# Places of weight and operand tiles modulo 512 bytes in stage 3, and a wait of GpSimd at the end of stage 2

## The reference

```python
def _cross_attention(q_in, kv_in, wq, bq, wk, bk, wv, bv, wo, bo, bias_k, bias_v):
    qh = (q_in @ wq + bq).reshape(b, q_len, H, K)      # H = 16, K = 128
    kh = (kv_in @ wk + bk).reshape(b, t, H, K)
    vh = (kv_in @ wv + bv).reshape(b, t, H, K)
    kh = jnp.concatenate([kh, bias_k], axis=1)         # one learned key and value
    vh = jnp.concatenate([vh, bias_v], axis=1)
    weights = jax.nn.softmax(jnp.einsum('bqhk,bthk->bhqt', qh, kh) / scale, axis=-1)
    ctx = jnp.einsum('bhqt,bthk->bqhk', weights, vh).reshape(b, q_len, H * K)
    return ctx @ wo + bo

x = res + _cross_attention(layer_norm(x), ctx, ...)    # twice, with other weights
x = x + gelu(layer_norm(x) @ w_fc1 + b_fc1, approximate=False) @ w_fc2 + b_fc2
```

## Time and profile before

| | us |
|---|---|
| median of 3 runs | 2145.59 |
| lowest, highest | 2144.91, 2145.69 |
| the profiled execution | 2143.41 |
| its span, first to last instruction | 2141.6 |
| TensorE matmuls busy in it | 1947.6 (91%) |
| VectorE, ScalarE, GpSimd busy | 1270.5, 1187.8, 675.5 |

### The profile page before, as it was taken

One profiled execution on the slowest core, in us unless ns is written; L12 is line 12 of the kernel. 1 busy time (PEld: TensorE's weight loads), 2 busy tenths in 40 slices (PEclk: granted clock), 3 DMA queues, 4 the chain that ended last, 5 costly groups with the idle time before them and its releaser, 6 DMA issues.

```text
span 2141.6 us, 43183 instructions
## 1 busy us (share of the span) xinstructions
PE 1947.6 (91%) x14880; PEld 1693.5 (79%) x14880; DVE 1270.5 (59%) x4126; ACT 1187.8 (55%) x3882; POOL 675.5 (32%) x613
## 2 busy tenths in 40 slices
PE   4678899999999989859999999999899999999889
PEld 3457777777777777648899999998799999999778
DVE  3577797878788864435555555556555555455653
ACT  2367887878787777526444444443644444444531
POOL 1233444444434343233222221223312222122452
PEclk8799999999999999979999999999999999999999
DMA  6000000000000000000000000000000000000100
GB/s 257 8 9 6 7 12 1 12 4 4 4 4 4 2 1 28 7 10 21 26 16 24 24 20 15 24 15 26 11 26 15 24 24 20 15 20 0 40 11 30
DMA packets 24635, 44.35 MB, mean 21 GB/s; under 512 B 2336, under 2 KB 12064, under 8 KB 23584
## 3 DMA queue, kind: packets, MB, share of 16 engines
q1 hardware_dynamic: 23328, 34.13, 5.2%
q10 hardware_dynamic: 1152, 8.26, 0.9%
HBM read 40.28 MB, written 2.10 MB: 20 GB/s over the span
## 4 chain that ended last, share of the span: by engine, by line
PE 49%; DVE 2%; ACT 2%; issue 1%; POOL 1%; ACTq 0%; DVEq 0%
PE general L1812 33%; PE o_psum L1867 6%; PE scores L1851 5%; PE pT_psum L1926 3%; PE scores L1977 1%; ACT probs L1457 1%; DVE oT L1634 1%; ACT oT L1473 1%; PE pT_psum L1977 1%; PE o_psum L1977 1%; POOL probs L1362 0%; PE general L1823 0%; DVE guess L1660 0%; ACT kT L1440 0%; ACT xhat L1430 0%
## 5 line engine op out<-in xcount | busy, mean ns | idle before, releaser
L515 POOL TENSOR_TENSOR probs<-probs,rsums 128x512 f32<-128x512 f32 (+1 forms) x288 | 283.1, 995 | 504.7 <-DVE rsums L740 504.1
L1362 POOL TENSOR_TENSOR probs<-probs,rsums 128x512 f32<-128x512 f32 x128 | 133.3, 1042 | 755.2 <-DVE rsums L1627 755.2
L561 ACT ACTIVATE probs<-negated,negmax 128x128 f32<-128x128 f32 (+1 forms) x768 | 325.5, 431 | 11.5 <-DVE negmax L731 11.1
L1465 ACT COPY probsT<-pT_psum 128x512 f32<-128x512 f32 x128 | 75.0, 586 | 295.8 <-PE pT_psum L1926 295.8
L1013 PE MATMUL pT_psum<-ident,probs 128*128 128x128 f32 x1088 | 176.4, 283 | 61.1 <-ACT probsT L569 30.3
L1013 PEld LDWEIGHTS pT_psum<-ident,probs 128*128 128x128 f32 x1088 | 124.7, 143 | 117.4 <-issue 69.8
L1812 PE MATMUL general<-w_o,oT 128*128 128x256 f32 x1536 | 200.4, 285 | 13.7 <-DVE oT L1634 13.7
L1812 PEld LDWEIGHTS general<-w_o,oT 128*128 128x128 f32 x1536 | 192.4, 192 | 22.3 <-DVE oT L1634 19.0
L1812 PE MATMUL general<-hT,w_qk 128*128 128x512 f32 x768 | 205.5, 403 | 1.5 <-POOL hT L1331 0.8
L1812 PE MATMUL general<-ctxT,w_qk 128*128 128x512 f32 x768 | 198.5, 394 | 2.9 <-DVEq L197 2.9
L1812 PEld LDWEIGHTS general<-w_v,ctxT 128*128 128x128 f32 x1536 | 192.3, 192 | 4.5
(11 more groups left out here) (186 smaller groups left out, 3891.0 us busy)
## 6 DMA issues: line engine op xcount, KB each, us to landing
raw_qk<-w_qk_dram SPq DMA_DIRECT2D x32, 256.0 KB, 2.8
weights_a<-weights_a_dram ACTq DMA_DIRECT2D x2, 2048.0 KB, 17.7
raw_v<-w_v_dram SPq DMA_DIRECT2D x16, 256.0 KB, 2.7
raw_vrows<-vrows_dram SPq DMA_DIRECT2D x16, 256.0 KB, 3.4
raw_o<-w_o_dram SPq DMA_DIRECT2D x16, 256.0 KB, 2.7
weights_a<-weights_a_dram ACTq DMA_DIRECT2D x3, 1024.0 KB, 9.9
X<-x_dram SPq DMA_DIRECT2D x8, 256.0 KB, 8.0
ctx_in<-ctx_dram SPq DMA_DIRECT2D x8, 256.0 KB, 2.8
```

The source lines that it names most:

```text
L515: nc.gpsimd.tensor_tensor(pr, pr, rsums[:, n % 4, 0:segs].unsqueeze(2).broadcast_to([P, segs, width(kind) // segs]), ALU.mult).then_inc(s[ ...
L561: last = nc.scalar.activation(probs[:, n % PROBS, i * wide:(i + 1) * wide], src[:, i * wide:(i + 1) * wide], ACT.Exp, scale=1.0 if kind == ...
L1362: nc.gpsimd.tensor_tensor(pr, pr, rsums[:, t % 2, :].unsqueeze(2).broadcast_to([P, NB, P]), ALU.mult).then_inc(s["probs_ready"], 1)
```

## The change

Two edits, shown whole below.

1. On GpSimd, ahead of the four low parts of ctxT, a wait for xhat_ready at the count of the last group's rms norm.
2. In EARLY_BUFFERS two unused tiles: `apart_v` of 48 floats (192 bytes) ahead of w_v, and `apart_o` of 80 floats (320 bytes) ahead of w_o. In stage 3 the six small tiles of 32 bytes each (192 bytes) are taken ahead of oT, probs and probsT rather than behind them.

```diff
@@ GpSimd, stages 0 to 2 @@
                 nc.gpsimd.tensor_tensor(early["vrow"][:, :], early["raw_vrows"][:, 0, :], early["raw_vrows"][:, 1, :], ALU.subtract).then_inc(late["vrow_ready"], 1)
+
+                wait_xhat(pool, "rms", GA - 1)
                 for i in range(B // NB):
                     at = slice(i * R, (i + 1) * R)
                     pool.wait_ge(late["ctxT_hi"], i + 1)
@@ EARLY_BUFFERS @@
-                 "raw_vrows": ([P, 2, 2 * P], F32), "w_qk": ([P, 2, 2, 2 * KC * P], F32R), "w_v": ([P, 2, KC * 2 * P], F32R), "w_o": ([P, 2, 2 * D], F32R),
+                 "raw_vrows": ([P, 2, 2 * P], F32), "w_qk": ([P, 2, 2, 2 * KC * P], F32R), "apart_v": ([P, 48], F32), "w_v": ([P, 2, KC * 2 * P], F32R), "apart_o": ([P, 80], F32), "w_o": ([P, 2, 2 * D], F32R),
@@ stage_3 @@
-        oT = sb("oT3", [P, 2, 2, B * P], F32R)
-        probs = sb("probs3", [P, 2, BANK])
-        probsT = sb("probsT3", [P, BANK])
         rawmax = sb("rawmax3", [P, 2, NB])
         negmax = sb("negmax3", [P, 2, NB])
         sums = sb("sums3", [P, 2, NB])
         learned = sb("learned3", [P, 2, NB])
         totals = sb("totals3", [P, 2, NB])
         rsums = sb("rsums3", [P, 2, NB])
+        oT = sb("oT3", [P, 2, 2, B * P], F32R)
+        probs = sb("probs3", [P, 2, BANK])
+        probsT = sb("probsT3", [P, BANK])
```

## The result

| | before | changed |
|---|---|---|
| median, us | 2145.97 (6 runs, 2144.91 to 2147.97) | 2132.18 (6 runs, 2127.27 to 2137.34) |
| ratio to before | | 0.9935 (0.992 to 0.995) |
| the profiled execution, us | 2143.41 | 2134.43 |
| its span | 2141.6 | 2132.5 |

13.8 us less. I had forecast 2114.7 in a range of 2105 to 2141: the direction is right, but the gain is less than half of the 30.9 us that I forecast, and the time lies outside the 2106 to 2128 that I gave the likeliest case; only the wider range, which reached down to "the places change nothing", holds it. In all medians and ratios of this document two runs far off the others are left out, one of the kernel before at 2525 us and one of `places_only` at 8678 us. Rows of the changed kernel with L numbers above 534 stand two to four lines further down than before.

What follows compares the result with a forecast made beforehand. TensorE, busy 91% of 2141.6 us, was taken as the bound. From the median 2145.59 us, 7.9 for the wait and 23.0 for the places came off, giving 2114.7 us, range 2105 to 2141.

Steps and rivals of the forecast that it cites:

- the likeliest case: Both parts work, the wait giving 7.9 us and the places 23.0: 2114.7 us, own range 2106 to 2128, chance 48%.
- The wait: Handover between stages: VectorE's four tiny instructions take 0.78 us in place of 8.70, so 7.92 us are gained.
- GpSimd's parts were hidden: Handover: the four ctxT parts, run later from about 930.9 to 940.1, have 12 us of cover before the stage ends.
- all of it moves by the same 7.92 us: Handover: transposes, copies and both matrices of the small layer, up to the stage's end, come 7.92 us earlier.
- The places: TensorE's 3456 matmuls of 256 columns with w_v, w_o and the last layer: 6.7 ns less each, 23.0 us.
- Only where load and stream are about equally long: TensorE's matmuls: an extra 6.7 ns each time was claimed for 256 columns, at 120.0 ns against 113.3.
- Rival 1: The new places change nothing and only the wait counts: 2137.7 us, chance 28%.
- Rivals 2, 3, 4: Worse places, 5 ns lost, 2155.0 us (10%); load freed, 108 ns, 2096.7 us (8%); wait without effect, 2122.6 us (3%).
- My last sign of being wrong: The prediction is wrong if the pitch of matmuls that the change doesn't touch changes.
- The cover of 0.25 us in the fourth step: Stage 3: GpSimd's probabilities end 0.25 us before TensorE's transposes; w_v shrinks by 0.16 us, at most 2.6 us lost.
- The clock: Handover: 2 us less or more of TensorE's low-clock stretch, worth about 1 us either way, zero in the sum.

Runs made afterwards that it cites:

- places_only: The changed kernel without the new wait on GpSimd, only the new places of the tiles: 2139.25 us, ratio 0.9973 to the kernel before.
- places_table: Not the kernel's computation: copies x and times groups of 24 matmuls at moved tile distances; 256 columns took 113.3 ns at distance 64, 120.0 at 0.
- history: Not the kernel's computation: 24 matmuls of 256 columns at eight distances, each behind five lead-ins; distance 64 gave 113.4 ns behind one, 117.8 behind others.

## Why the prediction was wrong, point by point

- **The wait: right, within the noise.** The chain of four went from 8.70 to 0.80 us where I had 0.78, TensorE's idle to 5.36 where I had 5.3. Alone the wait gives 6.4 us (ratio 0.9971, interval 4.3 to 8.4 us) against my 7.9. GpSimd's parts were hidden, as foretold. That GpSimd's parts held VectorE is shown by the pair of experiments: the stall is there whenever they run beside the four instructions and gone when they don't. That "all of it moves by the same 7.92 us" is not quite so: 7.15 us at the handover, and some 1.3 us more in stage 3's first twelve matmuls, both by the granted clock. Together the profiles give 8.5 us, the medians 6.4, with 7.9 between them and inside the interval.
- **The places: that they matter was right, the price was wrong.** The step that failed is "I take the whole 6.7 ns as what the new places return: 3456 x 6.7 ns = 23.0 us". The pitch fell by 2.5 ns with w_v (119.7 to 117.2) and 1.9 with w_o (119.6 to 117.7). 3456 by the mean of the two is 7.6 us; stage 3 became 7.1 us shorter behind its 31st matmul, the runs with the places alone 6.9 us. 113.3 was the right floor: nothing at 256 columns settled below it, and it is reached with the right distance and the right work ahead. My error was to take "not at the same place" for enough. Distance 128 costs as much as 0 and 160 nearly as much, most others lie between, and at the two used here there are two outcomes, of which the kernel mostly gets the worse (53 and 57 of 63 runs with w_v in its two profiles). That two reads meet was my picture of it; no run here shows reads, and that part of the cause stays open.
- **"Only where load and stream are about equally long": wrong.** `places_table` has 512-column matmuls at 226.7 ns with equal places and up to 234.2 with others. The long ones depend on the distance too, by as many ns, the other way round.
- **The row that I read too simply.** In the earlier trace rows the first w_v matmul has 278 ns and those behind it settle at 283: I read this as a price that can be avoided. The row also has two states of one shape in it, and I didn't ask which one a run settles in at a new distance. That this can depend on what ran before only `history` shows.
- **Rival 1 (places change nothing): wrong.** By the Trainium skill's rule in "SBUF — State Buffer", "Who interferes with whom", that TensorE's two reads are independent and never wait, the pitch would not depend on the places. Here it does, by up to 5.6%: 120.0 against 113.3 ns for the same 24 instructions with one tile moved by 64 bytes. My ground for the rival, that 512-column matmuls with equal places ran at 113.3 per 256 columns, was a true row that says nothing of 256 columns: equal places are the best for the one width and among the worst for the other.
- **Rivals 2, 3, 4: wrong.** No placement in the kernel made the 256-column matmuls slower than equal places, none went below 113.3, and the wait does what it says. My last sign of being wrong, that the pitch of untouched matmuls changes, did not come: the scores stay at 111.7 ns, hT with w_qk at 230.3 and 230.1, ctxT with w_qk at 227.9 and 228.6. The cover of 0.25 us in the fourth step held. The same two rows as the earlier trace rows, of the changed kernel, GpSimd's and TensorE's:

```profile
1330.67 1.04 POOL L1366 TENSOR_TENSOR probs<-probs,rsums 128x512 f32<-128x512 f32 x1 [6.79 <-DVE rsums L1631]
```

```profile
1331.91 0.60 PE L1930 MATMUL pT_psum<-ident,probs 128*128 128x128 f32 x4
```

GpSimd ends at 1331.71, the transposes start at 1331.91 and show no wait; the margin is 0.20 us.
- **The clock.** I allowed for the clock at the handover only, 2 us of low stretch. That was too little for a single execution: the first 135 us alone put the changed kernel's profile 4 to 5 us behind. Over several runs this averages out only slowly, as the spread of 2127 to 2137 us shows.

## What to carry to other kernels

When an engine with tiny instructions shows one that takes more than ten times its usual time, look for what its neighbour issues in just that stretch: a wait of one line on work that nobody needs yet was worth 6.4 us here. When TensorE is the bound and each matmul loads its own weights, measure the pitch against the distance of the two tiles' first bytes in a small kernel, before padding by guess; here a stand-in of the step with both distances moved named the best padding of those tried, which beat the change by another 4 to 6 us. And take a floor seen in a few records as a bound, not as the expected value: ask first how often the kernel would be in that state.

## What the runs showed of the hardware that I had not expected

- The pitch of 256-column fp32r matmuls with a load each depends on the two tiles' distance modulo 256 bytes, from 113.3 to 120 ns and a little over; that of 512-column ones from 226.7 to 234 ns, with equal places (and 16 bytes to either side) best.
- At distances 64 and 192 the same instructions on the same bytes settle at 113.3 or at 117.8 ns, depending on what TensorE ran before, and not on the twelve matmuls just ahead alone. Why was not tried further; the records show pitches, not the reads.
- 128-column and plain fp32 matmuls showed no dependence at the five distances tried.
- The stall of VectorE beside GpSimd's parts is nearly whole for the instructions that it hits: four of 0.16 us took 1.77 to 2.27 us each beside parts of 2.31. The two aggregates beside the same parts took their usual 0.25 us.
